# First weights of a mixture of experts loaded in 112 + 15 rows instead of 127, their repeated row in 128, and what the first unit needs put in front

## What is computed

```
x = x + 0.5 * moe(layernorm(x))            # 8 experts, hidden 512, top 2, w1, b1, w2, b2, router
x = x + rwkv(layernorm(x))
x = x + 0.5 * moe(layernorm(x))            # the same weights
x = x + 0.5 * quantised_ffn(layernorm(x))
x = x + attention(rms_norm(layernorm(x)))  # 16 heads of 64
x = x + 0.5 * quantised_ffn(layernorm(x))
moe: h = relu(x @ w1[e] + b1[e]); y = h @ w2[e] + b2[e]; out = sum over e of gate[:, e] * y[e]
```

## Time and profile before

| | |
|---|---|
| median of 3 runs | 2288.65 us |
| lowest and highest | 2284.3 and 2289.0 us |
| the profiled execution | 2287.96 us |
| its span in the profile | 2286.2 us |
| busy share of TensorE matmul, VectorE, GpSimd, ScalarE | 87%, 78%, 68%, 64% |
| mean granted clock of TensorE | 0.975 |
| DMA bytes, mean rate | 96.76 MB, 42 GB/s |

### The profile page before, as it was taken

How to read it: one execution, slowest core, us unless ns; L and a number is a source line. 1 busy time by engine, 2 the same in 40 slices (tenths; PEclk the granted TensorE clock), 3 DMA queues, 4 the chain that set the end, 5 groups by cost and what they waited for, 6 DMA issues and landing times. The chain is left out here.

```text
span 2286.2 us, 25543 instructions
## 1 busy us (share of the span) xinstructions
PE 1996.4 (87%) x8290; PEld 1421.5 (62%) x8290; DVE 1782.5 (78%) x1964; ACT 1457.9 (64%) x1800; POOL 1543.3 (68%) x767
## 2 busy tenths in 40 slices
PE   1007998899986899999999999999999999999877
PEld 1005776667855576676676766667667667666544
DVE  0005778877655789989989988989998998999785
ACT  0005555554442578877878877878787887887753
POOL 0004233322230589989999998999998998999872
PEclk9999999999987899999999999999999999999987
DMA  1112110112004012312303213123032131230000
GB/s 41 43 47 54 47 33 25 32 38 50 26 14 114 0 40 46 66 20 63 73 13 70 50 36 66 32 52 73 15 69 45 41 67 27 54 71 16 5 1 19
DMA packets 78758, 96.76 MB, mean 42 GB/s; under 512 B 31875, under 2 KB 35379, under 8 KB 78248
## 3 DMA queue, kind: packets, MB, share of 16 engines
q1 hardware_dynamic: 78630, 95.13, 18.2%
HBM read 43.18 MB, written 1.42 MB: 20 GB/s over the span
## 5 line engine op out<-in xcount | busy, mean ns | idle before, releaser
L598 POOL TENSOR_TENSOR p_l<-p_raw,p_h 128x1024 fp32r<-128x1024 f32 x512 | 1240.9, 2452 | 146.0 <-ACT p_h L1246 130.7
L1243 ACT ACTIVATE p_raw<-ps 128x1024 f32<-128x1024 f32 x512 | 566.8, 1107 | 243.1 <-PE ps L870 242.2
L1570 DVE TENSOR_REDUCE m_part<-ps 128x1 f32<-128x1024 f32 x480 | 584.5, 1218 | 126.0 <-PE ps L847 125.0
L1246 ACT ACTIVATE p_h<-ps 128x1024 fp32r<-128x1024 f32 x512 | 523.0, 1021 | 0.0
L869 PE MATMUL ps<-qa,ka 128*128 128x512 f32 x1024 | 445.8, 435 | 2.0 <-ACT m_t L1214 2.0
L870 PE MATMUL ps<-qb,kb 65*128 65x512 f32 x1024 | 409.6, 400 | 0.0
L884 PE MATMUL ps<-p_h,v_hl 128*128 128x512 f32 x1024 | 403.2, 394 | 1.1 <-POOL p_l L598 0.7
L1564 DVE TENSOR_REDUCE l_sum<-p_raw 128x128 f32<-128x1280 f32 x256 | 377.0, 1476 | 0.4
L847 PE MATMUL ps<-ka,qa 128*128 128x512 f32 x960 | 314.5, 409 | 12.2 <-DVE m_part L1570 11.8
L887 PE MATMUL ps<-p_l,v_hl 128*64 128x512 f32 x1024 | 321.6, 395 | 0.0
L1550 DVE TENSOR_REDUCE p_raw<-p_raw 128x128 f32<-128x1024 f32 x256 | 308.9, 1208 | 12.8 <-ACT p_raw L1243 12.8
(11 more groups left out here) (206 smaller groups left out, 2551.7 us busy)
## 6 DMA issues: line engine op xcount, KB each, us to landing
g_bc<-g_scratch SPq DMA_DIRECT2D x64, 256.0 KB, 3.6
xn<-r_scratch SPq DMA_DIRECT2D x59, 256.0 KB, 4.1
qa<-qk_hi SPq DMA_DIRECT2D x112, 128.0 KB, 2.4
ka<-qk_hi SPq DMA_DIRECT2D x56, 128.0 KB, 2.4
kb<-qk_hi SPq DMA_DIRECT2D x56, 128.0 KB, 2.4
ka<-xn SPq DMA_DIRECT2D x28, 128.0 KB, 2.3
qb<-xn SPq DMA_DIRECT2D x28, 128.0 KB, 2.4
ka<-qk_low SPq DMA_DIRECT2D x28, 128.0 KB, 2.7
```

The lines of the kernel that those rows point to most:

```text
L598: nc.gpsimd.tensor_tensor(p_l[:, g % 4, :, :], slots(g), p_h[:, g % 4, :, :].bitcast(fp32), ALU.subtract).then_inc(pl_done, 1)
L1243: af(slots(g), s_t, ACT.Exp).then_inc(raw_done, 1)
L1246: af(p_h[:, g % 4, :, :], s_t, ACT.Exp).then_inc(ph_done, 1)
L1570: nc.vector.tensor_reduce(m_part[:, it, half:half + 1], ps[:, 4:6, :].rearrange("p b n -> p (b n)"), AX.X, ALU.max).then_inc(s_max, 1)
```

## The change

Each part's rows 0 to 126 of w1 are loaded by two transfers, rows 0 to 111 and rows 112 to 126; row 127 is repeated into all 128 partitions of `w1_base` in place of 127 (the last one is not read). VectorE now waits for three transfers of a part, 48, not 32. The loads of w2 become a function of their own, `load_second_weights`. SP's new order: x chunk 0, first weights of part 0, b1, router weights, router bias, b2, wait for `const_row`, row of ones, w2 of part 0, first weights of part 1, wait for `b1_done`, bias row, w2 of part 1, x chunk 1, first weights of part 2, w2 of part 2, x chunks 2 and 3, first weights of part 3, w2 of part 3, weights of the second block. The first two entries of `WEIGHTS_AT` move from -8 and -5 to -6 and -2.

```diff
--- before.py
+++ after.py
@@ -70,7 +70,8 @@
 NORMS = ((0, 0), (0, 1), (0, 2), (1, 0), (0, 3), (1, 1), (2, 0), (1, 2), (2, 1), (1, 3), (2, 2), (2, 3))
 ROUTE_AT = (-16, 0, 20, 59, 95, 131, 167, 187)
 RWKV_AT = (40, 76, 112, 148)
-WEIGHTS_AT = (-8, -5, 2, 6, 10, 14, 18, 22)
+WEIGHTS_AT = (-6, -2, 2, 6, 10, 14, 18, 22)
+MOST = 112
 WEIGHT_PARTS = ((0, 1), (1, 2), (2, 4), (4, 8))
 N_MEAN, N_CEN, N_SQR, N_VAR, N_STD, N_REC, N_SPREAD, N_OUT = 0, 1, 1, 4, 5, 6, 8, 9
 R_HIGH, R_LOGITS, R_LOW, R_TOP, R_SECOND, R_EXP, R_GATES, R_TURN, R_ROWS = 10, 11, 11, 12, 13, 14, 15, 18, 19
@@ -337,27 +338,36 @@
             def load_weights(i):
 
                 lo, hi = WEIGHT_PARTS[i]
-                sp.dma_start(w1_raw[0:C - 1, lo:hi, :], a["w1T"][0:C - 1, lo:hi, :]).then_inc(w1_loaded[i], 16)
-                sp.dma_start(w1_base[0:C - 1, lo:hi, :],
-                             a["w1T"][C - 1:C, lo:hi, :].to_broadcast([C - 1, hi - lo, H0])).then_inc(w1_loaded[i], 16)
+                for rows in (slice(0, MOST), slice(MOST, C - 1)):
+                    sp.dma_start(w1_raw[rows, lo:hi, :], a["w1T"][rows, lo:hi, :]).then_inc(w1_loaded[i], 16)
+                sp.dma_start(w1_base[:, lo:hi, :],
+                             a["w1T"][C - 1:C, lo:hi, :].to_broadcast([C, hi - lo, H0])).then_inc(w1_loaded[i], 16)
+
+            def load_second_weights(i):
+
+                lo, hi = WEIGHT_PARTS[i]
                 sp.dma_start(w2_raw[:, lo:hi, :, :], a["w2T"][:, lo:hi, :, :]).then_inc(w2_loaded[i], 16)
 
             load_x(0)
+            load_weights(0)
             sp.dma_start(b1[:, :], a["b1T"].rearrange("p e a -> p (e a)")).then_inc(b1_loaded, 16)
-            sp.wait_ge(const_row, 1)
-            sp.dma_start(x_h[C - 1:C, :].bitcast(fp32), h_l[0:1, :, :].rearrange("p a n -> p (a n)").bitcast(fp32)).then_inc(row_loaded, 16)
-            load_weights(0)
             sp.dma_start(rw[:, :], a["router_w"]).then_inc(small_loaded, 16)
             sp.dma_start(rb[:, :], a["router_b"].rearrange("(a e) -> a e", a=1).to_broadcast([128, E])).then_inc(small_loaded, 16)
             sp.dma_start(b2[:, :], a["b2T"]).then_inc(small_loaded, 16)
+            sp.wait_ge(const_row, 1)
+            sp.dma_start(x_h[C - 1:C, :].bitcast(fp32), h_l[0:1, :, :].rearrange("p a n -> p (a n)").bitcast(fp32)).then_inc(row_loaded, 16)
+            load_second_weights(0)
             load_weights(1)
+            sp.wait_ge(b1_done, 1)
+            sp.dma_start(w1_raw[C - 1:C, :, :].rearrange("p e n -> p (e n)"), b1_row[:, :]).then_inc(b1_moved, 16)
+            load_second_weights(1)
             load_x(1)
             load_weights(2)
+            load_second_weights(2)
             for c in range(2, NC):
                 load_x(c)
             load_weights(3)
-            sp.wait_ge(b1_done, 1)
-            sp.dma_start(w1_raw[C - 1:C, :, :].rearrange("p e n -> p (e n)"), b1_row[:, :]).then_inc(b1_moved, 16)
+            load_second_weights(3)
             sp.dma_start(rwkv_w[:, :, :], a["rwkv_wT"]).then_inc(rwkv_loaded, 16)
             sp.dma_start(mix[:, :], a["mix"]).then_inc(rwkv_loaded, 16)
             sp.dma_start(gamma1[:, :], a["gamma"]).then_inc(l1_loaded, 16)
@@ -1368,7 +1378,7 @@
             def base_weights(t):
                 for e, base in enumerate(WEIGHTS_AT):
                     if t - base == W_BASE:
-                        dve.wait_ge(w1_loaded[[e < hi for _, hi in WEIGHT_PARTS].index(True)], 32)
+                        dve.wait_ge(w1_loaded[[e < hi for _, hi in WEIGHT_PARTS].index(True)], 48)
                         tt(w1_raw[0:C - 1, e, :], w1_raw[0:C - 1, e, :], w1_base[0:C - 1, e, :], ALU.subtract).then_inc(w1_ready, 1)
 
             def norm(k, c, at, out):
```

## The result

| | before | changed |
|---|---|---|
| median, lowest, highest of 4 runs, us | 2286.48, 2282.75, 2289.00 | 2129.14, 2127.88, 2132.42 |
| ratio, 95% interval | | 0.9315, 0.9296 to 0.9334 |
| profiled execution, its span | 2287.96, 2286.2 | 2127.88, 2126.1 |
| first product | 179.91 | 19.83 |
| gates turned (PE L737, now L747) | 185.06 | 26.50 |

The account below looks back on a forecast made before the run. The prediction took 127-row weight loads on one DMA engine at 27 GB/s to bound the first 180 us. 2286.2 - 160.0 + 1.0 gave 2127.2 us of span, hence 2130 us; the range 2124 to 2145 held 0.79.

Parts of the forecast that it names:

- What bounds the start: First 180 us: 127-row loads of w1 and its repeated row, 4.06 MB on one DMA engine at 27 GB/s, 150 us.
- Part 1: Loads of w1: 112 rows run like 128-row transfers, 170 to 400 GB/s; 15 rows matter little, 1.1 to 4.4 us.
- Part 2: Start: b1, now behind three transfers, lands at about 6.5 us and costs the whole chain 1.1 us.
- Part 3: Start of the first unit: first product at 19.95 us, not 179.91, so 160.0 us earlier; bias row hidden.
- Part 4: Routing after the layer norm: gates ready at 24.8, turned at 25.1, covered by 0.3 us; nothing added, maybe 1 or 2.
- Part 5: Remaining weights and gates: all landed at about 35 us, first gate in time by 0.2 us; 1 us of stall taken.
- The sum: Whole kernel: 2286.2 - 160.0 + 1.0 = 2127.2 us of span, 2130 us predicted, 6.9% less.
- Nothing spreads: Rival on the loads: split parts run one after the other at the old rate, 20 us gained, 2270 us; chance 0.02.
- 112 rows do not spread: Rival on the w1 loads: one engine carries 1.83 MB, 50 us stall at tick 8, 2180 us; chance 0.06.
- The clock rival: Rival on TensorE: late weights make it stop and start at the lower clock, 2295 us or so; chance 0.03.

Follow-up runs that it names:

- the order alone: The changed kernel with w1 and its repeated row loaded in 127 rows again, VectorE waiting for 32: 2264.26 us in one run.
- b1 first: The changed kernel with b1 issued right behind x chunk 0, ahead of the first weights: 2131.87 us, ratio 0.9336.
- four extra loads: The changed kernel with four more 1 MB transfers of part 3's repeated row between the weights and the gates: 2137.48 us, ratio 0.9338.
- old ticks: The changed kernel with the first two entries of WEIGHTS_AT back at -8 and -5: 2128.99 us, ratio 0.9327.
- spreading alone: The kernel before with only w1 cut into 112 + 15 rows and the repeated row in 128, VectorE waiting for 48: 2145.17 us, ratio 0.9395.

## Why the prediction was right

The predicted 2130 us stand against 2129.14. By its own steps:

- **What bounds the start.** Right: one DMA engine at 27 GB/s. (127 rows twice are 4.16 MB in the trace's units, not 4.06, so 154 us, not 150; no other step uses it.) With 113 rows it is back, with 112 gone; the first product of the order alone, at 50.3, shows that the order doesn't remove it.
- **Part 1.** Right for 112 rows. For 15 rows either bound would have done.
- **Part 2, b1 1.1 us later.** It came at 6.46, predicted 6.5; putting b1 first took 0.9 us back.
- **Part 3, the first product at 19.95.** Measured 19.83. The bias row, predicted near 13 and needed at 16.6, was issued at 8.74, landed 2.1 us later and cost no wait.
- **Part 4, the routing covered by 0.3 us.** The term was mis-sized. The chain of the two largest took 4.6 us (17.93 to 22.55), not 2.83, and the gates were turned at 26.50, not 25.1: 1.4 us lost, which the text allowed for ("1 or 2 us") but did not add. The 2.83 came from a stretch in which GpSimd was idle; in the new place it was not. The gates' own 3.2 us came from a stretch with GpSimd at work, and were 3.4.
- **Part 5, weights at 35 us, 1 us of stall for the gates.** The mechanism was right, as the four extra loads show, the size too high: the weights were there at 30.8, and no stall came. The whole repeated row was priced at the 174 GB/s of the gates' broadcasts, which have 2 KB pieces; half of its bytes come in pieces of 8 KB, and such transfers ran at 428 GB/s in the run with the four extra loads. The mean over all loads was 280 GB/s from 10 to 20 us and 311 from 20 to 30 (258 and 278 in the second profile).
- **The sum.** Part 4's loss of 1.4 us and part 5's 1.0 us that didn't come nearly cancel. The first gated output is 158.3 us earlier, the last 157.1; the profiled execution then happened to be 3.0 us quicker in its unchanged rest. The near hit is partly luck: the nine executions of this kernel lie between 2122.93 and 2132.53.
- **The rivals.** "Nothing spreads" and "112 rows do not spread" were made to happen and gave 2264 and 2189, where the text had 2270 and 2180. The clock rival did not come. After the gap TensorE was at the lower level for some 3 us, as before, and for some 7 in the second profile; its matmuls also took 0.63 us from the first product to 23.6, as they had before to 184.2. In the first profile that is no more than before, in the second some 5 us more at the slow level, which costs half of it and not 160 us.

## What to carry to other kernels

When the DMA rate of a long stretch is that of one engine, look at the row counts of the loads: 127 and 113 rows ran on one engine, 112 and 128 spread, and cutting a load into a multiple of 16 and a rest was worth 138 us here, the order 18 more. Before moving work to the front, ask what else the same queue carries: here a start 130 us earlier bought 19 us by itself, because the gates stood behind the loads. And when a chain is moved out of an idle stretch, its durations must be taken beside the work that will run next to it.

## What the hardware showed that was not expected

- VectorE's small operations with both inputs in SBUF ended just behind the GpSimd operation beside them, 0.97 to 1.32 us for 0.19. The same 13 operations took 4.6 us here and 2.83 us before, when GpSimd was idle.
- In all seven traces in which TensorE had a gap of 1.8 to 2.2 us before the variances of chunk 1 (before, changed twice, b1 first, old ticks, spreading alone, four extra loads), its clock was at 0.50 soon after, for about 3 us in four and about 7 in three. In the three with a gap of 0.2 to 0.7 us it stayed at 1.00.
- A granted clock of 1.00 ahead of a trace's first clock record is no reading. In the changed kernel the records begin at 23.6 us, in its second profile at 25.5, in the kernel before at 184.2. From the first product up to there, matmuls of 512 columns took 0.63 us with the column at 1.00, and 0.39 from there on. So TensorE began each time at the slow level, and the mean clocks do not count it.
- One DMA engine moved 26 to 27 GB/s. Sixteen on mixed loads from HBM reached 258 to 311 GB/s over 10 us, and 409 from 26 to 30 us, nearly sixteen times the one. The gates' broadcasts, 128 copies of one 2 KB row, ran at only 174, but copies of an 8 KB row at 428.
